# A layered kernel on one core: the routed layer chooses its experts by raw logits, and steps and dataless matmuls are placed anew

## The chip, the core and the metric

One Trainium2 chip, of which the kernel uses 1 core. The metric is the device time of one execution in microseconds (us). Before the change it is 2814.28 us, the median of 3 runs (2812.36 to 2824.87).

The engines are named PE (TensorE, matmuls; PEld is its weight load), DVE (VectorE), ACT (ScalarE), POOL (GpSimd) and SP (SyncE, here only DMA issues).

## What is computed

For each of 16 sequences of 256 tokens by 128 features, two layers with two parts each: a selective scan, a routed feed-forward part, a gated delta rule, and attention with a dense mixture of 8 experts. The change is in the routed part:

```
logits = X @ routing_W.T + expert_bias            # 8 per token
activation = sqrt(softplus(logits))
top_vals, top_idx = top_k(activation, 2)
combine = sum(one_hot(top_idx) * top_vals)        # 8 coefficients per token, two of them not zero
hdn = silu(X @ rW1[e] + rb1[e]);  y = hdn @ rW2[e] + rb2[e]
out = shared(X) + sum_e combine[e] * y[e]
```

Softplus and square root both rise with their argument, so the two largest activations belong to the two largest logits.

## The kernel before, in words

A sequence is one item: its 256 tokens are two tiles of 128 partitions. The work of an item is a list of named steps in two halves. The first half (x) has the scan (names a_), the routed part (b_) and the projections of the delta rule (c_norm to c_roots). The second half (y) has the delta rule's pair products (c_logd, c_prod), the inversion of two triangular blocks in five levels (lev_T, lev_Z, lev_TT, each for two chunks), its application (c_R to c_res), the attention (d_) and the experts (d_up, d_down, d_mix).

`follow` runs the first half of item 0 alone, then a loop of 15 iterations, each with the first half of item i and the second half of item i-1 interleaved, and then the second half of the last item alone. Every engine has its own program and keeps its own strict order. In the loop the order is a string of x and y, `TURNS`: each letter takes the next step of its half. Engines wait for one another through semaphores (`Signal`, with `at(i, k)` as the count to wait for).

`WARM` names steps of PE ahead of which `keep_warm` issues that many matmuls of constants into a bank that nobody reads, before the step's first wait. They compute nothing that is used.

Steps that matter here. On the DVE: `b_logits2` (L1416) adds the bias to the logits and makes -|x| for the softplus; `softplus16` (L1298) makes log(1+exp(-|x|)) in 13 small dependent steps, each waiting for the one before, after ACT's exp; `b_select` (L1423) takes the largest values (`max`), their indices (`max_index`), turns them to floats, and makes the 8 coefficients from four picks and a sum; `b_coef` copies the turned coefficients. On POOL `b_root_` (L560) takes the square root of all 16 softplus columns as a power, and `power` (L530) makes the roots of the norms. Both `b_` and the delta rule's `c_beta`/`c_soft2` use the same softplus code.

The order of the DVE around it: c_rms, b_logits, b_soft2, c_gated, b_select, c_res, b_coef, d_norm. PE's: b_logits, c_turn_o (turns what c_gated made), c_out (projects it; c_res needs it), b_coef (turns the coefficients), b_up. ACT copies between c_turn_o and c_out.

Of the kernel before, what the change touches and what calls it, by code (L numbers as in the profile page):

```python
# [9 lines left out]
ALU = mybir.AluOpType  # L10
# [15 lines left out]
E0 = 8  # L26
# [88 lines left out]
for e in range(E1):  # L115
    EXPERTS += [("d_down", e, 0), ("d_down", e, 1)]
    if e + 2 < E1:
# [11 lines left out]
        "yyyyyxyxyyyyyyxxyyyyyxyyyyxyxyyyxyxyyyyxxyyyxxyyxxyyxxyxyxxyxxxxyxyxxyyxxxxyxxxyyxyyyxyyxyyxxyyy"  # L129
        "yyxyxyyyyxyyxyyxyyxyyxyyyxxyyyxxxyyyyyyyxx"),  # L130
    "vector": (
        "xyxyyyxyyxyyxyyyyxxyyyxyyxyyxyyxyyxyyxyyxyyxyyxxyxyxxxyxyxxxxxxyxyxxyxyxxyxyxyxxyxxxyxyyxxxyyyxy"
        "xxxyxxxxyxyxxxyxyxxyyyy"),
    "scalar": (
        "yyxxyyxxxxxyyyxyyyyyxxyyxyyxyxxxyxxyxxxyxxyyyxyxyyxxyxyxyyxyyxxyyxyxyxxxyyxyxyxyyxxx"),
    "gpsimd": (
        "yyxxyyyyyyxxxxxxxxxxyyxyxxx"),
# [4 lines left out]
    ("a_xproj",): 2, ("a_out",): 2, ("b_turn",): 1, ("b_logits",): 1, ("c_prod", 2, 0): 1, ("c_prod", 2, 1): 1,  # L142
    ("lev_Z", 0, 0): 2, ("lev_TT", 0, 0): 2, ("lev_Z", 1, 0): 1, ("lev_TT", 1, 0): 2, ("lev_TT", 1, 1): 1,
    ("lev_Z", 2, 1): 2, ("lev_TT", 2, 0): 1, ("lev_TT", 2, 1): 2, ("lev_Z", 3, 1): 2, ("lev_TT", 3, 0): 2,
    ("lev_TT", 3, 1): 1, ("lev_Z", 4, 1): 1, ("lev_TT", 4, 0): 3, ("lev_TT", 4, 1): 1, ("c_X", 0): 3, ("c_O", 0): 1,
    ("c_S",): 1, ("c_kS",): 1, ("c_top", 1): 1, ("c_low", 1): 1, ("c_O", 1): 2, ("c_turn_o",): 2, ("c_out",): 1,
    ("d_scores",): 2, ("d_turn_p",): 1, ("d_av",): 1, ("d_a",): 2,
# [16 lines left out]
def build(nc, a, out, NB):  # L164
    with ExitStack() as ctx:
# [107 lines left out]
        topf = sb("topf", [P, TILES, 8])  # L273
        pick = sb("pick", [P, TILES, 2, E0])
# [99 lines left out]
        b_lgp = sig("b_logits_ps"); b_lg = sig("b_logits"); b_sel = sig("b_select", 4); b_root = sig("b_root")  # L374
# [19 lines left out]
        c_tp = sig("c_top_ps", 2); c_tx = sig("c_top", 2); c_lp = sig("c_low_ps", 2); c_low = sig("c_low", 2)  # L394
        c_X = sig("c_X_ps", 2); c_U = sig("c_U", 2); c_Uw = sig("c_Uw")
# [4 lines left out]
        d_qk = sig("d_qk_ps"); d_qks = sig("d_qk", 2); d_vp = sig("d_v_ps"); d_v = sig("d_v")  # L400
# [113 lines left out]
        def _(g):  # L514
# [94 lines left out]
        def _(s):  # L609
# [58 lines left out]
            def sp_exp(i, which):  # L668
                s.wait_ge(sp_in.h, sp_in.at(i, which + 1))
                s.activation(sp[:, 1, :], sp[:, 1, :], ACT.Exp).then_inc(sp_e.h, 1)  # L670
# [133 lines left out]
        def _(t):  # L804
# [246 lines left out]
            def c_top(i, ch):  # L1051
# [10 lines left out]
                last.then_inc(c_tp.h, 1)  # L1062

            def c_low_(i, ch):
# [6 lines left out]
                last.then_inc(c_lp.h, 1)  # L1071

            def c_X_(i, ch):
# [5 lines left out]
                last.then_inc(c_X.h, 1)  # L1079
# [130 lines left out]
        def _(v):  # L1210
# [205 lines left out]
            def b_logits2(i):  # L1416
# [4 lines left out]
                softplus16_in(i, 0, lg2)  # L1421

            def b_select(i):  # L1423
                v.wait_ge(b_root.h, b_root.at(i, 1))
# [4 lines left out]
                v.wait_ge(b_sel.h, b_sel.at(i, 1))  # L1429
                v.tensor_copy(*carrier)  # L1430
# [41 lines left out]
            def c_beta(i):  # L1472
# [5 lines left out]
                softplus16_in(i, 1, lg2)  # L1478
# [5 lines left out]
            def c_soft2(i):  # L1484
                softplus16(i, 1, lg2)
# [101 lines left out]
            def c_low_(i, ch):  # L1587
                v.wait_ge(c_lp.h, c_lp.at(i, ch + 1))
# [158 lines left out]
```

## Time and profile before

| | |
|---|---|
| median of 3 runs | 2814.28 us |
| the profiled execution | 2817.26 us, span 2815.5 us |
| mean granted TensorE clock | 0.931 |
| PE busy | 2434.8 us (86%), 22584 matmuls |
| DVE busy | 2208.3 us (78%) |
| ACT busy | 1197.7 us (43%) |
| POOL busy | 605.6 us (22%) |

The span is the time from the first to the last instruction. The clock is given as a share of full speed: 1.00 is 2.4 GHz, 0.50 is 1.2 GHz. A line of a timeline has the start in us from the span's start, the time in us, engine, line of the kernel, operation, what is written and read, how many such instructions follow one another (a line with x4 merges four), and in brackets how long the engine sat idle before it and who released it. The loop's iterations are all alike, so one of them is read, the one whose DVE part starts at 1171.60 us.

### The profile page before, as it was taken

The page shows a single profiled execution, that of the slowest core. Times are in us where ns is not written, and L with a number is a line of the kernel's source. Part 1 is how long each engine was busy: PE and PEld are TensorE (multiplying, and loading weights), DVE is VectorE, ACT ScalarE, POOL GpSimd, SP SyncE. Part 2 cuts the span into 40 slices and gives each one's busy share as a digit, 9 for nine tenths or more (in the row PEclk, how much of TensorE's full clock was granted, in tenths as well). Part 3 has the DMA queues.
Part 4 walks back from the last instruction along what each step waited for, and adds up shares of the span by engine and source line. Part 5 has one row for each costly group of instructions (what it writes and reads, how often), then busy time and mean ns, then how long its engine had stood idle before and what let it go on. Part 6 is the DMA issues. An engine that isn't in the chain of part 4 may idle for free.

```text
span 2815.5 us, 60867 instructions
## 1 busy us (share of the span) xinstructions
PE 2434.8 (86%) x22584; PEld 1890.6 (67%) x22584; DVE 2208.3 (78%) x5056; ACT 1197.7 (43%) x2697; POOL 605.6 (22%) x465
## 2 busy tenths in 40 slices
PE   4688989888898888989888898988889888898987
PEld 2466767667686766768667686766768666676875
DVE  6677887878879787887978779787887978788742
ACT  3233536435263542536444253543526354353612
POOL 2122221221322122231222222122131212223100
PEclk7689999989999999999999999999999999999987
DMA  4000000000000000000000000000000000000000
GB/s 132 4 2 3 7 4 1 8 3 7 3 7 2 3 8 3 7 4 1 8 3 8 3 7 4 1 8 3 7 3 7 2 3 8 3 7 2 1 6 2
DMA packets 24831, 21.41 MB, mean 8 GB/s; under 512 B 7217, under 2 KB 21570, under 8 KB 24530
## 3 DMA queue, kind: packets, MB, share of 16 engines
q1 hardware_dynamic: 24530, 17.26, 2.2%
q8 instruction: 205, 3.36, 0.5%
q14 instruction: 96, 0.79, 0.1%
HBM read 15.13 MB, written 2.13 MB: 6 GB/s over the span
## 4 chain that ended last, share of the span: by engine, by line
issue 42%; PE 25%; DVE 23%; POOL 6%; ACT 1%; DVEq 0%; POOLq 0%; ACTq 0%
PE banks L1048 4%; PE banks L887 3%; PE banks L1020 3%; DVE wide L1390 3%; PE banks L1012 2%; DVE wide L1398 2%; DVE inv L1560 2%; POOL lg L562 2%; DVE inv L1564 2%; DVE wide L1378 2%; POOL rq L534 2%; PE banks L1001 1%; PE banks L1040 1%; DVE inv L1551 1%; PE banks L864 1%
## 5 line engine op out<-in xcount | busy, mean ns | idle before, releaser
L558 POOL TENSOR_TENSOR wide<-wide 128x512 f32<-128x512 f32 x128 | 215.3, 1682 | 782.0 <-DVE wide L1398 428.4
L1513 DVE SCALAR_TENSOR_TENSOR wide<-pad,conv,wide 128x256 f32<-128x256 f32 x864 | 369.5, 492 | 0.0
L1390 DVE TENSOR_TENSOR_SCAN wide<-wide 128x1024 f32<-128x1024 f32 x128 | 294.3, 2300 | 1.9 <-ACT wide L664 0.3
L1040 PE MATMUL banks<-hideb,identb 128*128 128x512 bf16 x800 | 276.1, 402 | 0.0
L1184 PE MATMUL banks<-inv,up 128*128 128x256 f32 x1024 | 265.9, 391 | 0.0
L1194 PE MATMUL banks<-down,inv 128*128 128x128 f32 x2048 | 257.2, 277 | 0.0
L1194 PEld LDWEIGHTS banks<-down,inv 128*128 128x128 f32 x2048 | 250.7, 192 | 5.9
L1020 PEld LDWEIGHTS banks<-inv 64*64 64x64 f32 x5120 | 164.4, 136 | 111.4 <-issue 111.4
L792 ACT ACTIVATE inv<-banks,up1b 128x256 f32<-128x256 f32 x512 | 206.7, 481 | 65.0 <-PE banks L1184 63.3
L1020 PE MATMUL banks<-inv 64*64 64x64 f32 x5120 | 182.2, 222 | 57.8 <-DVE inv L1564 57.8
L664 ACT ACTIVATE wide<-small,a_neg 128x255 f32<-128x255 f32 x512 | 214.4, 496 | 35.7 <-DVE wide L1390 35.5
L1184 PEld LDWEIGHTS banks<-inv,up 128*128 128x128 f32 x1024 | 184.6, 193 | 21.0 <-issue 0.2
L745 ACT COPY inv<-banks 128x512 f32<-128x512 f32 x160 | 91.3, 580 | 242.0 <-DVE inv L1560 209.5
L1020 PEld LDWEIGHTS banks<-inv,mats 64*64 64x64 f32 x5120 | 163.8, 136 | 35.4 <-issue 35.4
L1020 PE MATMUL banks<-inv,mats 64*64 64x64 f32 x5120 | 180.6, 221 | 4.6 <-DVE inv L1557 4.6
L1378 DVE TENSOR_TENSOR wide<-banks,small 128x1024 f32<-128x1024 f32 x128 | 154.2, 1205 | 3.4 <-PE banks L864 3.4
L534 POOL TENSOR_TENSOR vscale<-vscale,expo 128x16 f32<-128x16 f32 x16 | 46.3, 2895 | 506.8 <-DVE rq L1522 506.8
L1398 DVE TENSOR_TENSOR wide<-banks,wide 128x1024 f32<-128x1024 f32 x128 | 154.2, 1204 | 1.0
L1689 DVE SCALAR_TENSOR_TENSOR inv<-banks,gt,inv 128x128 f32<-128x128 f32 x256 | 77.1, 342 | 98.9 <-PE banks L1194 98.9
L864 PE MATMUL banks<-bc,sel3b 96*128 96x256 bf16 x512 | 100.5, 285 | 55.9 <-DVE wide L1378 31.4
L968 PEld LDWEIGHTS banks<-ones_col,wide 128*128 128x128 f32 x1024 | 135.0, 200 | 9.4 <-issue 2.2
L887 PE MATMUL banks<-wide,con 128*128 128x512 f32 x256 | 138.6, 634 | 0.3 <-POOL wide L558 0.3
(277 smaller groups left out, 4846.7 us busy)
## 6 DMA issues: line engine op xcount, KB each, us to landing
gates_bc<-gate_rows SPq DMA_DIRECT2D x32, 128.0 KB, 2.9
x<-in_x SPq DMA_DIRECT2D x16, 128.0 KB, 2.1
up<-in_W SPq DMA_DIRECT2D x1, 2048.0 KB
out<-xn_y SPq DMA_DIRECT2D x16, 128.0 KB, 2.0
wide<-in_wmod SPq DMA_DIRECT2D x2, 384.0 KB, 5.3
con<-in_con SPq DMA_DIRECT2D x1, 724.0 KB, 4.5
w_k<-in_Wk SPq DMA_DIRECT2D x1, 512.0 KB
w_q<-in_Wq SPq DMA_DIRECT2D x1, 512.0 KB
```

The costliest lines, as they stand in the source:

```text
L558: g.tensor_tensor(ypart[p % 2], r[:, 0:512], r[:, 512:1024], ALU.add).then_inc(a_yp.h, 1)
L664: last = s.activation(decay[st % 2][:, at + 1:at + T], dt[:, c, 1:T], ACT.Exp, scale=a_neg[:, c, st * SG + q:st * SG + q + 1])
L792: s.activation(hm[e % 2][:, m, :], bank(3 + half, T, q * T), ACT.Relu, bias=up1b[:, HB1 * e + m:HB1 * e + m + 1]).then_inc(d_hid.h, 1)
L887: t.matmul(bank(2), ident, ypart[st % 2], start=st == 2, stop=st == NG + 1).then_inc(a_yq.h, 1)
L1020: last = t.matmul(PS[a:b, out, h * HALF:(h + 1) * HALF], weights(h, a, b), values(h, a, b), start=True, stop=True)
L1040: t.matmul(bank(bk), identb[:], hideb[:].unsqueeze(1).broadcast_to([P, HG, P]), start=True, stop=True)
L1184: last = t.matmul(bank(3 + half, T, q * T), up1[:, e, m * P:(m + 1) * P], xxT, start=True, stop=True)
L1194: last = t.matmul(bank(bk, D, j * D), hm[e % 2][:, m, j * P:(j + 1) * P], down1[:, HB1 * e + m, :], start=m == 0, stop=m == HB1 - 1)
L1378: v.tensor_tensor(drive[st % 2].rearrange("p (q c t) -> p q c t", q=SG, c=CB), bank(0).rearrange("p (q t) -> p q t", t=T).unsqueeze(2).bro ...
L1390: v.tensor_tensor_scan(state[st % 2], decay[st % 2], drive[st % 2], 0.0, ALU.mult, ALU.add).then_inc(a_h.h, 1)
L1398: v.tensor_tensor(r, bank(1).rearrange("p (q t) -> p q t", t=T).unsqueeze(2).broadcast_to([P, SG, CB, T]), r, ALU.mult).then_inc(a_rd.h, 1)
L1513: v.scalar_tensor_tensor(dst, src, w, dst, ALU.mult, ALU.add).then_inc(c_conv.h, 1)
```

## The change

The routed part's softplus and root are no longer taken of all 16 logits of a partition (2 tiles x 8), but of the 4 chosen ones (2 x 2). `max` is run on the logits themselves in `b_logits2`; the two largest of each tile are copied into `chosen`, whose -|x| goes to ACT; the indices are found and made floats in the same step, ahead of the softplus. The softplus steps take their width as an argument (4 here, 16 for the delta rule as before). POOL's power writes 4 values into `topv`, and `b_select` keeps only picks and sum.

`TURNS` and `WARM` are new for all engines: 50 dataless matmuls per iteration become 45. A few semaphores are merged (`c_slv` for `c_tp`, `c_lp`, `c_X`; `d_qkv_ps` for two), with the same events behind each wait.

```diff
             def b_root_(i):
-                g.tensor_tensor(lg[:]..., sp[:, 0, :], expo[:, 1:2].broadcast_to([P, TILES * E0]),
+                g.tensor_tensor(topv[:]..., sp[:, 0, 0:2 * TILES], expo[:, 1:2].broadcast_to([P, 2 * TILES]),
...
             def b_logits2(i):
                 v.wait_ge(b_lg.h, b_lg.at(i, 1))
-                softplus16_in(i, 0, lg2)
-
-            def b_select(i):
-                v.wait_ge(b_root.h, b_root.at(i, 1))
                 v.tensor_copy(*carrier)
                 for j in range(TILES):
                     last = v.max(top[:, j, :], lg[:, j, :])
                 last.then_inc(b_sel.h, 1)
                 v.wait_ge(b_sel.h, b_sel.at(i, 1))
+                v.tensor_copy(chosen[:].rearrange("p (j n) -> p j n", n=2), top[:, :, 0:2]).then_inc(b_sel.h, 1)
+                v.wait_ge(b_sel.h, b_sel.at(i, 2))
+                softplus_in(i, 0, chosen[:], 2 * TILES)
                 v.tensor_copy(*carrier)
                 for j in range(TILES):
                     last = v.max_index(topi[:, j, :], top[:, j, :], lg[:, j, :])
                 last.then_inc(b_sel.h, 1)
-                v.wait_ge(b_sel.h, b_sel.at(i, 2))
+                v.wait_ge(b_sel.h, b_sel.at(i, 3))
                 v.tensor_copy(topf[:], topi[:]).then_inc(b_sel.h, 1)
-                v.wait_ge(b_sel.h, b_sel.at(i, 3))
+
+            def b_select(i):
+                v.wait_ge(b_root.h, b_root.at(i, 1))
+                v.wait_ge(b_sel.h, b_sel.at(i, 4))
                 for j in range(TILES):
                     for n in range(2):
-                        last = v.tensor_scalar(pick[:, j, n, :], ..., topf[:, j, n:n + 1], top[:, j, n:n + 1],
+                        last = v.tensor_scalar(pick[:, j, n, :], ..., topf[:, j, n:n + 1], topv[:, j, n:n + 1],
                                                ALU.is_equal, ALU.mult)
```

What the new strings do to the order of the loop, engine by engine (steps not named keep their places):

```
DVE   start:      c_prod 0 1 ahead of a_norm2; a_zgate ahead of c_prod 2 1, a_silu2 ahead of c_prod 3 1
      inversion:  before: a_split a_soft Z00 Z01 T10 a_step T11 Z10 scan0 Z11 T20 read0 T21 Z20 scan1 ...
                  after:  a_split Z00 Z01 a_soft T10 T11 Z10 Z11 a_step T20 T21 scan0 Z20 read0 Z21 T30 scan1 ...
      attention:  d_v ahead of b_up 4
      end:        d_mix 4 behind c_scales
PE    inversion:  scan0 behind TT11 (was behind Z10), read0/scan1 behind TT20, read1/scan2 behind TT30
      attention:  d_turn ahead of b_up 2, d_qkv ahead of b_up 3, d_scores ahead of b_up 5
      end:        d_down 5 1 ahead of c_turn_k 1; c_turn_v ahead of d_down 7
ACT   inversion:  x_kept and the level 0 copy of chunk 0 ahead of a_soft; its chunk 1 ahead of scan0 and scan1
      later:      scan7 ahead of c_S; d_turn and d_qkv one step earlier among b_up
POOL  no step that has work is moved
```

(Z01 is lev_Z of level 0, chunk 1; T is lev_T and TT is lev_TT.)

The counts of `WARM` that change, per iteration: fewer at a_xproj, a_out, c_O 1, d_scores (2 to 1 each), c_X 0 (3 to 1), c_kS and d_turn_p (1 to 0), c_turn_o (2 to 0), lev_Z 0 0, 2 1 and 3 1 (2 to 1), lev_Z 4 1 (1 to 0), lev_TT 0 0 and 1 0 (2 to 0), 2 1 and 3 0 (2 to 1), 4 0 (3 to 2); more at b_turn (1 to 2), c_X 1 and c_turn (0 to 1), d_turn and c_prod 3 1 (0 to 2), lev_Z 0 1 (0 to 2), 1 0 (1 to 2), 2 0 and 4 0 (0 to 1), 3 0 (0 to 3), lev_TT 3 1 (1 to 2).

## Rows read from the trace of the kernel before

**Rows 1.** Windows by stage: us, busy of PE, PEld, DVE, ACT, POOL, clock, DMA.

```profile
1190.00:1226.00 36.00, 30.26 (x662) 22.85 (x662) 34.81 (x45) 17.13 (x34) 3.82 (x3) 1.00 0.01 3
...
1290.00:1310.00 20.00, 20.00 (x126) 18.07 (x125) 19.49 (x57) 16.94 (x43) 1.45 (x1) 1.00 0.00 1
```

**Rows 2.** Timeline of the DVE, the logits (L1418) of five items.

```profile
421.14 0.17 DVE L1418 TENSOR_TENSOR lg<-banks,rout_b 128x16 f32<-128x16 f32 x1 [1.83 <-PE banks L906]
...
589.60 0.17 DVE L1418 TENSOR_TENSOR lg<-banks,rout_b 128x16 f32<-128x16 f32 x1 [1.36 <-PE banks L906]
...
758.19 0.17 DVE L1418 TENSOR_TENSOR lg<-banks,rout_b 128x16 f32<-128x16 f32 x1 [1.58 <-PE banks L906]
...
924.80 0.17 DVE L1418 TENSOR_TENSOR lg<-banks,rout_b 128x16 f32<-128x16 f32 x1 [1.58 <-PE banks L906]
...
2597.19 0.17 DVE L1418 TENSOR_TENSOR lg<-banks,rout_b 128x16 f32<-128x16 f32 x1 [1.58 <-PE banks L906]
```

**Rows 3.** Windows at the low clock (0.50), columns as in rows 1.

```profile
667.60:670.90 3.30, 3.20 (x6) 1.72 (x7) 0.96 (x6) 0.60 (x1) 0.25 (x1) 0.50 0.20 50
756.40:766.40 10.00, 5.05 (x19) 3.32 (x19) 5.42 (x29) 1.36 (x3) 6.30 (x2) 0.50 0.00 0
...
1258.10:1271.60 13.50, 8.86 (x28) 5.67 (x29) 8.90 (x42) 1.69 (x4) 6.47 (x3) 0.50 0.00 0
```

**Rows 4.** Timeline of the DVE, logits to coefficients.

```profile
1259.08 0.17 DVE L1418 TENSOR_TENSOR lg<-banks,rout_b 128x16 f32<-128x16 f32 x1 [1.58 <-PE banks L906]
...
1259.74 0.17 DVE L1308 TENSOR_SCALAR sp<-sp 128x16 f32<-128x16 f32 x1 [0.28 <-ACT sp L670]
...
1263.27 0.69 DVE L1631 TENSOR_TENSOR inv<-inv,gnw 128x512 f32<-128x512 f32 x1
1266.02 0.15 DVE L1425 COPY carried<-con 128x1 f32<-128x1 f32 x1 [2.06 <-POOL lg L562]
...
1267.03 0.87 DVE L1439 TENSOR_SCALAR pick<-con,topf,top 128x8 f32<-128x8 f32 x4
1267.93 0.18 DVE L1443 TENSOR_TENSOR cf<-pick 128x16 f32<-128x16 f32 x1
```

**Rows 5.** Timeline of POOL, three powers.

```profile
1254.25 0.71 POOL L534 TENSOR_TENSOR mv_x<-mv_x,expo 128x2 f32<-128x2 f32 x1 [6.04 <-DVE mv_x L1265]
...
1257.58 2.90 POOL L534 TENSOR_TENSOR rms<-rms,expo 128x16 f32<-128x16 f32 x1 [1.01 <-DVE rms L1623]
1262.59 3.40 POOL L562 TENSOR_TENSOR lg<-sp,expo 128x16 f32<-128x16 f32 x1 [2.10 <-DVE sp L1318]
```

**Rows 6.** Timeline of PE, c_turn_o, c_out and b_coef.

```profile
1264.01 1.11 PE L1104 MATMUL banks<-con,inv 128*128 128x128 f32 x4 [4.10 <-DVE inv L1631]
...
1265.80 2.08 PE L1112 MATMUL banks<-w_o,inv 128*128 128x128 f32 x8 [0.25 <-ACT inv L757]
1268.17 0.60 PE L929 MATMUL banks<-con,cf 128*9 128x128 f32 x2 [0.29 <-DVE cf L1443]
```

**Rows 7.** Timeline of PE, between b_out and d_turn_p.

```profile
1281.99 0.39 PE L1040 MATMUL banks<-hideb,identb 128*128 128x512 bf16 x1
1282.21 0.60 PE L1137 MATMUL banks<-con,inv 128*128 128x128 f32 x4
```

**Rows 8.** Timeline of PE, c_turn_v at the loop's end.

```profile
1334.05 0.60 PE L984 MATMUL banks<-con,wide 128*128 128x128 f32 x4
```

**Rows 9.** Timeline of the DVE, the last d_mix and the loop's restart.

```profile
1334.34 0.61 DVE L1689 SCALAR_TENSOR_TENSOR inv<-banks,gt,inv 128x128 f32<-128x128 f32 x2 [1.18 <-PE banks L1194]
...
1338.83 0.49 DVE L1259 BATCH_NORM_STATS2 stats_x<-x 128x6 f32<-128x128 f32 x2 [2.58 <-issue]
```

**Rows 10.** Timeline of the DVE, the loop's start and the inversion's first level.

```profile
1173.64 0.59 DVE L1271 TENSOR_SCALAR xn_x<-x,mv_x 128x128 f32<-128x128 f32 x2
...
1176.30 0.61 DVE L1541 SCALAR_TENSOR_TENSOR mats<-banks,negc,inv 128x128 f32<-128x128 f32 x2 [0.30 <-PE banks L1012]
...
1196.15 0.72 DVE L1560 STREAM_TRANSPOSE inv<-banks 128x512 f32<-128x512 f32 x1 [0.73 <-PE banks L1020]
```

More of the change, by code:

```diff
@@ L128 @@
     "tensor": (
-        "yyyyyxyxyyyyyyxxyyyyyxyyyyxyxyyyxyxyyyyxxyyyxxyyxxyyxxyxyxxyxxxxyxyxxyyxxxxyxxxyyxyyyxyyxyyxxyyy"
-        "yyxyxyyyyxyyxyyxyyxyyxyyyxxyyyxxxyyyyyyyxx"),
+        "yyyyyxyxyyyyyyxxyyyyyyyyxyyyxxyyyyxxyyxyxyyyxxyyxxyyxxyxyxxyxxxxyxyxxyyxxxyxyxxyxxyyyxyyxyyxxyyy"
+        "yyxxyyyyyxyyxyyxyyxyyxyyyxyxyyxxyxyyyyxyyx"),
     "vector": (
-        "xyxyyyxyyxyyxyyyyxxyyyxyyxyyxyyxyyxyyxyyxyyxyyxxyxyxxxyxyxxxxxxyxyxxyxyxxyxyxyxxyxxxyxyyxxxyyyxy"
-        "xxxyxxxxyxyxxxyxyxxyyyy"),
+        "xyyxyyxyxyyxyyyyyxyyxyyyyxyyxyxyyxyxyyxyxyyxyyxxyxyxxxyxyxxyxxxxxyxxyxyxxyxyxyxxyxxyxxyyxxxyyyxy"
+        "xxxyxxxxyxyxxxxyxxyyyyy"),
     "scalar": (
-        "yyxxyyxxxxxyyyxyyyyyxxyyxyyxyxxxyxxyxxxyxxyyyxyxyyxxyxyxyyxyyxxyyxyxyxxxyyxyxyxyyxxx"),
+        "yyxxyyxxyyxyxxyyxyxyyyxyyyxxxyyxxxxyxxyxyxxxyyyxyyxxyxyxyyxyyxyxxyxyxyyxyxyxyxxyyxxx"),
     "gpsimd": (
-        "yyxxyyyyyyxxxxxxxxxxyyxyxxx"),
+        "yyxyyyyyyxxxxxxxxxxxyyxyxxx"),
 }
 WARM = {
[L142 to L147, printed above, removed]
+    ("a_xproj",): 1, ("a_out",): 1, ("b_turn",): 2, ("b_logits",): 1, ("c_turn",): 1, ("c_prod", 2, 0): 1,
+    ("c_prod", 2, 1): 1, ("c_prod", 3, 1): 2, ("lev_Z", 0, 0): 1, ("lev_Z", 0, 1): 2, ("lev_Z", 1, 0): 2,
+    ("lev_TT", 1, 1): 1, ("lev_Z", 2, 0): 1, ("lev_Z", 2, 1): 1, ("lev_TT", 2, 0): 1, ("lev_TT", 2, 1): 1,
+    ("lev_Z", 3, 0): 3, ("lev_Z", 3, 1): 1, ("lev_TT", 3, 0): 1, ("lev_TT", 3, 1): 2, ("lev_Z", 4, 0): 1,
+    ("lev_TT", 4, 0): 2, ("lev_TT", 4, 1): 1, ("c_X", 0): 1, ("c_O", 0): 1, ("c_S",): 1, ("c_top", 1): 1,
+    ("c_low", 1): 1, ("c_X", 1): 1, ("c_O", 1): 1, ("c_out",): 1, ("d_turn",): 2, ("d_scores",): 1, ("d_av",): 1,
+    ("d_a",): 2,
 }
@@ L669, in sp_exp @@
                 s.wait_ge(sp_in.h, sp_in.at(i, which + 1))
-                s.activation(sp[:, 1, :], sp[:, 1, :], ACT.Exp).then_inc(sp_e.h, 1)
+                n = (2 * TILES, TILES * NH)[which]
+                s.activation(sp[:, 1, 0:n], sp[:, 1, 0:n], ACT.Exp).then_inc(sp_e.h, 1)
             def b_up_(i, m):
@@ L1078, in c_X_ @@
                     last = t.matmul(PS[HALF:P, 3 + ch, h * DV:(h + 1) * DV], TTd[ch][HALF:P, h, :], R[HALF:P, h, :], start=True, stop=True)
-                last.then_inc(c_X.h, 1)
+                last.then_inc(c_slv.h, 1)
             def c_O_(i, ch):
@@ L1698, in _ @@
                            b_norm=lambda i: norm(i, 1), b_norm2=lambda i: norm2(i, 1), b_logits=b_logits2,
-                           b_soft2=lambda i: softplus16(i, 0, lg2), b_select=b_select, b_coef=b_coef, b_up=b_up_, b_res=b_res,
+                           b_soft2=lambda i: softplus(i, 0, chosen[:], 2 * TILES), b_select=b_select, b_coef=b_coef, b_up=b_up_, b_res=b_res,
                            c_norm=lambda i: norm(i, 2), c_norm2=lambda i: norm2(i, 2), c_beta=c_beta, c_soft2=c_soft2,
```

52 lines of the change are left out of this document (27 added, 25 removed).

## The prediction

> **What bounds the kernel now.** I read the DVE and PE timelines of one period of the loop first, then the same period in windows by stage. In the inversion stage the DVE is busy 34.81 of 36.00 us, in the experts' stage PE is busy for all of 20.00 us and the DVE for 19.49 [rows 1]. So the DVE sets the pace from the loop's start to the end of the scan, PE sets it through the experts, and in the 30 us between the two a chain of small steps does: logits, softplus, root, choice, residual, attention. The reader is to see that an order changed inside a stage whose bound has no idle time can only keep or lose time.
>
> Second, the start of the routed layer's logits (L1418) in each iteration [rows 2]. From the 5th to the 15th iteration of the loop it comes (2597.19 - 924.80) / 10 = 167.24 us apart, while 421.14 to 589.60 is 168.46 and 758.19 to 924.80 is 166.61. Third, where TensorE's clock is at its low level, 1.2 GHz [rows 3]: in a settled iteration it is low through 1258.1 to 1271.6, from just before the logits; the short iteration of 166.61 had its low stretch from 756.4 for only 10.0 us, 1.8 us before its logits; an early, long one had a second low stretch at 667.6. My reading: the place of an iteration against the clock's steps decides how much of its work is slow, and lateness is partly given back. That is worth up to 167.24 - 166.61 = 0.63 us per iteration.
>
> The sentences on a page: the Trainium skill, "TensorE: Matmul & The Clock Gate", section "Part 1: The HAM clock gate (the "warmup" mystery)", says that the activity window that decides the clock runs free of the kernel. The steady 167.24 after unequal first periods agrees; taken as a strict rule it would hold the loop at exactly 167.24, which is the second rival below.
>
> **The change part by part.**
>
> Routed choice, before: logits at 1259.08, softplus steps from 1259.74 (0.28 of it a wait for ACT's exp), c_gated ends at 1263.27 + 0.69 = 1263.96, the DVE then waits 2.06 for the root and runs the choice from 1266.02 to 1267.93 + 0.18 = 1268.11 [rows 4]. After: maximum, index and cast (1267.03 - 1266.02 = 1.01) move ahead of the softplus steps, with one new small copy; a small dependent step is about 0.21 from start to start, so logits, copy and minus-absolute value are 0.63. Softplus starts 1.64 after the logits instead of 0.66: 0.98 later, and ACT's exp hides in it. Its 13 steps get 4 columns for 16. No row of before has these steps at 4 columns; the bounds are 0 and, for lack of a nearer row, a saving of 0.02 each, and I take 0.01, 0.1 in all. c_gated thus ends 0.9 later, at 1264.86.
>
> The power on POOL: 16 columns take 2.90 where nothing disturbs it and 3.40 here, 2 columns 0.71 [rows 5]. For 4 I take an estimate on the line between, 0.71 + 2 x 2.19 / 14 = 1.0 (bounds 0.7 and 2.9). It runs beside c_gated's 1.4, so the 2.06 wait vanishes. Of the choice, picks and sum are left, 1268.11 - 1267.03 = 1.08: the coefficients are ready at 1265.95, 2.15 earlier.
>
> What is late next: PE turns c_gated's result (1.11), ACT copies it, c_out takes 2.08 and ends at 1267.88; then PE waited 0.29 for the coefficients [rows 6]. All of this now ends 0.9 later, 1268.78. On the DVE c_res stands between choice and b_coef and waits for c_out: it starts at 1268.80 instead of 1268.11, and b_coef and d_norm behind it. So the 2.15 gained turns into 0.7 lost here. Two things give it back: PE has no gap before b_coef any more, so the high clock may come back earlier, and d_turn and d_qkv are put ahead of b_up's later blocks. I walk it through the rows to b_out, which needs the last hidden block: it starts within 0.3 of where it did. I take 0; bounds -0.5 (clock back earlier) and +0.7.
>
> The dataless matmuls: ahead of d_turn_p the one at 1281.99, between b_out's end and the turn at 1282.21, goes: -0.2 on the path [rows 7]. The others lie in PE's waits; around c_kS, c_X and c_O a few of about 0.22 each are freed on PE where the DVE is the bound: 0. Whether their new places keep the clock high I can't price from before; it is the slower rival.
>
> The loop's end: the last d_down is followed by c_turn_v (four turns, 0.60, about 0.44 from start to start) [rows 8]; now c_turn_v goes first. The last d_mix starts as its matmuls end and the DVE restarts at 1338.83, with 2.58 of loop overhead, behind it [rows 9]. PE has no gap there, so the restart is 0.44 later: +0.4 (bounds 0 and 0.6).
>
> The loop's start: a_norm2 (1173.64) now follows one more c_prod step, 0.9 later; the wait of 0.30 at 1176.30, a PE product held up by that very step, partly pays for it. The convolution waits for the chain a_norm2, turn, a_in: +0.3 (bounds 0 and 0.9) [rows 10].
>
> The inversion: before, scan work filled the gaps between levels and the DVE waited 0.73 once (1196.15) [rows 10]. Now levels 0 and 1 run through before the scan begins. The 0.73 is what one such gap costs when a single transpose (0.72) stands where PE has a level's product to make. With nothing but the other chunk's transpose to cover it I take two gaps of 0.5 and 0.4 for level 1, estimates below that row. On ACT a_soft is now queued behind the copy for level 0, which waits for the DVE's transpose of level 1, so exp and log come later, and a_step waits for them, by another 0.4. 1.3 instead of 0.7: +0.6 (bounds -0.7, were all idle gone, and +1.2). The fused semaphores wait for the same events: 0. ACT's scans are in time for the DVE either way.
>
> Sum per iteration: 0 - 0.2 + 0.4 + 0.3 + 0.6 = +1.1, before the clock gives back 0.6: +0.5. Fifteen iterations of the loop: +7.5. Ahead of the loop the first routed layer runs alone, without c_gated behind the root: the change saves 3.4 - 1.0 there, some 2.5 once. After the loop, new places of dataless matmuls: 0, bounds -4 and +4. The profiled execution, span 2815.5, own time 2817.26, becomes 2822.3; the median of the runs stands 2.98 below it, so 2819.3, say 2819.
>
> **The rivals.**
>
> The choice's gain passes. If c_gated's chain is not last (PE at its high clock for c_turn_o and c_out: 1.11 + 2.08 would halve) and the new order of the inversion costs nothing, 2.15 per iteration goes: -32 - 2.5 gives 2780; half of it, 2797. For it: the root's wait is the longest of the DVE in that stage. Against: c_out ended only 0.2 before the DVE came to it.
>
> The loop holds its step. Periods return to 167.24 whatever the stages do, and only the first part's 2.5 is gained: 2812. For it: ten periods average 167.24 after three unequal ones [rows 2]. Against: a give-back of more than 0.63 was never seen.
>
> Slower: new low stretches. With the 50 dataless matmuls cut to 45 and put elsewhere, PE goes to its low level in a second place, as at 667.6 [rows 3], in every iteration. Price: 168.46 - 167.24 = 1.2 per iteration on top of the 0.5, or in place of the give-back: 1.2 to 2.3 times 15, +18 to +34, less 2.5: 2830 to 2846. It decides as soon as one such stretch stands in each period of the loop, or if my +1.1 isn't given back at all (+16.5 - 2.5: 2828).
>
> **How the numbers follow.** Forecast 2819 (its own range 2809 to 2827) 0.35; loop holds its step 0.20; slower 0.27; choice's gain passes 0.18. The bound of 0.5% (about what a measurement of this kernel can tell from no change) is 14 us: 2800 and 2828. Faster 0.18; same 0.54; slower 0.28, with a little of the forecast's upper end. For 8 in 10 the range takes in half of the faster case and most of the slower one: 2793 to 2838.
>
> **What would show it.** Right: no DVE wait at the routed choice; the DVE waits for PE (c_out) before c_res; waits of 0.3 to 0.5 behind the first transposes of level 1; a_soft's exp behind a copy on ACT; the last d_mix later by 0.4 from PE's last d_down; logits 167.2 to 167.8 apart. Wrong: logits under 166.5 apart with c_res starting at once (the gain passes), or a 0.50 stretch outside the one round the logits in a settled iteration (the slower rival). A power of 4 columns on POOL longer than 1.4 would bring back a wait ahead of the picks.

## The result, and the profile after

The changed kernel takes 2852.84 us, the median of 4 runs (2852.45 to 2857.18), beside 2813.34 us of the kernel before (4 runs, 2812.36 to 2824.87): ratio 1.0129, 95% interval 1.0108 to 1.0150. It is 1.3% slower where 0.2% was forecast, and beyond the range's upper end of 2838. The profiled execution took 2852.45 us.

The page of after, its span and the engines' busy time:

```profile
span 2850.7 us, 60783 instructions
...
PE 2441.0 (86%) x22504; PEld 1899.2 (67%) x22504; DVE 2216.5 (78%) x5072; ACT 1194.4 (42%) x2697; POOL 586.2 (21%) x465
```

Shares say nothing here: the DVE's busy time rose by 8 us and the span by 35. So I read one settled period of the loop, logits to logits, on the DVE, as before. Columns: start, time, engine, line, operation, and in brackets the idle time before and its releaser.

```profile
1442.31 0.17 DVE L1422 TENSOR_TENSOR lg<-banks,rout_b 128x16 f32<-128x16 f32 x1 [1.17 <-PE banks L910]
...
1443.68 0.16 DVE L1312 TENSOR_SCALAR sp<-sp 128x4 f32<-128x4 f32 x1
...
1446.99 0.69 DVE L1637 TENSOR_TENSOR inv<-inv,gnw 128x512 f32<-128x512 f32 x1
...
1447.94 0.87 DVE L1445 TENSOR_SCALAR pick<-con,topf,topv 128x8 f32<-128x8 f32 x4 [0.27 <-POOL topv L565]
...
1451.74 0.42 DVE L1290 TENSOR_TENSOR xn_y<-banks,gates_bc 128x256 f32<-128x256 f32 x1 [2.71 <-PE banks L1116]
...
1517.65 0.61 DVE L1695 SCALAR_TENSOR_TENSOR inv<-banks,gt,inv 128x128 f32<-128x128 f32 x2 [1.61 <-PE banks L1198]
...
1521.83 0.49 DVE L1263 BATCH_NORM_STATS2 stats_x<-x 128x6 f32<-128x128 f32 x2 [2.65 <-issue]
...
1525.56 1.73 DVE L1275 TENSOR_SCALAR xn_x<-x,mv_x 128x128 f32<-128x128 f32 x2
...
1549.77 0.69 DVE L1570 TENSOR_TENSOR inv<-banks,con 128x512 f32<-128x512 f32 x1 [0.73 <-PE banks L1024]
1550.71 0.69 DVE L1570 TENSOR_TENSOR inv<-banks,con 128x512 f32<-128x512 f32 x1 [0.24 <-PE banks L1024]
1551.56 0.69 DVE L1370 SCALAR_TENSOR_TENSOR small<-small 128x512 f32<-128x512 f32 x1 [0.17 <-ACT small L655]
...
1612.66 0.17 DVE L1422 TENSOR_TENSOR lg<-banks,rout_b 128x16 f32<-128x16 f32 x1 [1.17 <-PE banks L910]
```

The period is 1612.66 - 1442.31 = 170.35, against 167.24 in [rows 2]. Of the routed choice, the 2.06 us wait of [rows 4] is now 0.27, for POOL; but c_res, the next step shown, waits 2.71 for PE's c_out (L1116). c_gated ends 1446.99 + 0.69 - 1442.31 = 5.37 after the logits, against 4.88 in [rows 4]. The line to stop at is a_norm2 (L1275): its two instructions took 0.59 in [rows 10] and take 1.73. POOL's timeline of after, the power in the choice and then what stands beside a_norm2:

```profile
1446.31 1.51 POOL L565 TENSOR_TENSOR topv<-sp,expo 128x4 f32<-128x4 f32 x1 [2.19 <-DVE sp L1322]
...
1525.57 0.64 POOL L596 TENSOR_SCALAR_AFFINE_SELECT mats<-mats 128x512 f32<-128x512 f32 x1 [1.61 <-DVE mats L1547]
1526.18 1.04 POOL L584 TENSOR_TENSOR inv<-gl,con 128x512 f32<-128x512 f32 x1
```

Windows at the low clock in the same period (start:end, length, busy of PE, PEld, DVE, ACT, POOL, clock, DMA, GB/s):

```profile
1442.60:1452.60 10.00, 4.62 (x17) 3.34 (x17) 6.37 (x33) 0.79 (x2) 3.02 (x2) 0.50 0.00 0
1521.10:1524.40 3.30, 3.30 (x9) 2.62 (x8) 1.90 (x9) 0.60 (x1) 1.02 (x3) 0.50 0.05 12
1586.00:1589.20 3.20, 3.20 (x14) 2.61 (x13) 3.20 (x3) 1.08 (x3) 2.43 (x1) 0.50 0.03 5
```

In [rows 3] a settled iteration had one such stretch, round the logits. Now there are three: round the logits (shorter, 10.0 for 13.5 us), at the loop's restart, 79 us after the logits, and behind c_X 0, 144 us after them. Of the 14 full periods 11 have both the second and the third, and the other three have one in the inversion, 113 to 114 us after the logits.

The rest is told by stage. The table is worked out from the starts of DVE instructions in each trace, as medians over the 14 periods between the item 1 and item 15 logits. "prob" is the first step that uses the attention's probabilities, "split" is a_split. "Low stretch" is short for a stretch at the low clock. A second number behind a slash is the value in periods that have no further low stretch in that stage.

| kernel | period | logits to c_res | to prob | to last d_mix | to restart | to split | to c_R 0 | to logits |
|---|---|---|---|---|---|---|---|---|
| before | 167.30 | 9.03 | 12.49 / 11.95 | 53.97 | 4.19 | 18.95 | 34.98 | 33.55 |
| changed | 170.37 | 9.43 | 11.50 | 54.69 | 3.93 | 20.96 / 20.26 | 35.43 | 34.30 / 33.55 |
| e1_choice_only | 167.74 | 9.42 | 12.15 / 11.90 | 53.97 | 4.20 | 18.96 | 34.98 | 33.55 |
| e3_old_warm | 169.56 | 9.42 | 11.62 | 54.73 | 3.81 | 21.20 / 20.26 | 35.58 | 33.54 |
| f1_end_order | 167.30 | 9.38 | 11.90 | 54.54 | 3.97 | 18.95 | 34.99 | 33.56 |
| f2_inversion_order | 168.59 | 9.43 | 11.90 | 53.98 | 4.31 | 19.02 / 18.95 | 35.58 | 33.56 |
| g1_start_order | 170.28 | 9.42 | 11.90 | 53.97 | 4.22 | 21.28 / 20.26 | 36.10 | 33.15 |
| h2_changed_apart | 169.00 | 9.43 | 11.50 | 54.69 | 3.81 | 20.23 / 19.12 | 35.61 | 33.55 |
| h3_filled_inversion | 165.57 | 8.05 | 11.90 | 53.97 | 4.21 | 19.26 | 35.00 | 33.15 |

For before, the value behind the slash is that of periods whose low stretch round the logits is 10 us long and not 13.5. The 14 periods from the second logits to the last take 2383.57 us for 2344.70 (+38.9, or 2.8 each). What lies ahead of the second logits is 1.6 shorter, the tail behind the last 2.1, and 38.9 - 3.7 is the span's 35.2.

### The profile page after: what moved, and what is told of

The parts are those of the page before. It is cut to its first block, busy times and chain, and to the rows that moved or that the text cites. A ratio compares the mean times of both kernels' runs of the same rounds, so it can differ in the third digit from the quotient of the medians.

```text
span 2850.7 us, 60783 instructions
## 1 busy us (share of the span) xinstructions
PE 2441.0 (86%) x22504; PEld 1899.2 (67%) x22504; DVE 2216.5 (78%) x5072; ACT 1194.4 (42%) x2697; POOL 586.2 (21%) x465
## 4 chain that ended last, share of the span: by engine, by line
issue 38%; DVE 27%; PE 26%; POOL 4%; ACT 2%; DVEq 0%; POOLq 0%; ACTq 0%
PE banks L1052 4%; DVE wide L1394 3%; PE banks L891 3%; DVE wide L1402 3%; DVE inv L1566 2%; PE banks L1188 2%; PE banks L1198 2%; PE banks L1016 2%; DVE inv L1570 2%; DVE wide L1382 2%; DVE xn_x L1275 2%; POOL rq L537 1%; PE banks L1024 1%; DVE inv L1557 1%; DVE mats L1547 1%
## 5 line engine op out<-in xcount | busy, mean ns | idle before, releaser
L561 POOL TENSOR_TENSOR wide<-wide 128x512 f32<-128x512 f32 x128 | 226.0, 1766 | 778.6 <-DVE wide L1402 435.8
L1044 PE MATMUL banks<-hideb,identb 128*128 128x512 bf16 x720 | 260.3, 398 | 0.0
L1016 PE MATMUL banks<-kq 128*128 128x256 f32 x512 | 148.7, 424 | 0.1
```

Source lines behind the costliest of these rows:

```text
L561: g.tensor_tensor(ypart[p % 2], r[:, 0:512], r[:, 512:1024], ALU.add).then_inc(a_yp.h, 1)
L1044: t.matmul(bank(bk), identb[:], hideb[:].unsqueeze(1).broadcast_to([P, HG, P]), start=True, stop=True)
```

## The experiments

Each ratio is to the kernel before, run beside it on the same chip, with a 95% interval.

### Choice, orders and dataless matmuls taken apart

```diff
 e1_choice_only:  the changed kernel
-TURNS, WARM as changed
+TURNS, WARM as before
```

> The kernel before with the routed choice of the change alone: max on the raw logits, softplus and root on 4 columns, the old order of steps and the old dataless matmuls. Theory A (the new orders and the moved dataless matmuls cost the time, the choice is nearly neutral because c_gated's chain is 0.5 to 0.9 us later): within 6 us of before, periods of the loop 167.2 +- 0.2, no low-clock stretch outside the one round the logits. Theory B (the later c_gated alone pushes the loop out of its 167.24 us step): about 2850, periods near 170.6 with extra low-clock stretches. Theory C (the choice's 2.06 us wait is a real gain): 2785 or less, periods 165.5 or less.

```diff
 e2_orders_only:  the kernel before
-TURNS, WARM as before
+TURNS, WARM as changed
```

> The kernel before with the new order strings and the new counts of dataless matmuls, but the old choice (16 columns, root before the choice). Theory A: as slow as the changed kernel, 2845 to 2860, periods near 170.6, low-clock stretches at the loop's restart and in the application stage. Theory B (the choice is the cause): within 6 us of before. If choice and orders were tuned for each other: slower than the changed kernel by 2 us per iteration, 2880.

```diff
 e3_old_warm:  the changed kernel
-WARM as changed
+WARM as before
```

> The changed kernel with the old counts of dataless matmuls (50 for 45), new order and new choice kept. If the moved dataless matmuls let the clock fall (c_X 0 has 3 again where the changed kernel has a low stretch after it): the stretch after c_X 0 is gone, and the time falls towards 2815 to 2830. If the order of steps is the cause: within 6 us of the changed kernel, 2852.

```diff
 e4_old_turns:  the changed kernel
-TURNS as changed
+TURNS as before
```

> The changed kernel with the old order of steps, the new counts of dataless matmuls and the new choice kept. If the order of steps is the cause: within 6 us of before, 2813. If the dataless matmuls are the cause: a low-clock stretch after c_X 0 in each period and 2835 to 2855. If either alone is enough, both this and the kernel with the old counts stay near 2850; if only both together do it, both come out near 2813.

| kernel | median us | before beside it | ratio |
|---|---|---|---|
| e1_choice_only | 2818.60 | 2817.10 | 1.0004 (0.9989 to 1.0018) |
| e2_orders_only | 2850.25 | 2817.10 | 1.0110 (1.0085 to 1.0136) |
| e3_old_warm | 2847.52 | 2817.10 | 1.0102 (1.0077 to 1.0126) |
| e4_old_turns | 2860.99 | 2817.10 | 1.0152 (1.0128 to 1.0177) |

The new choice alone changes nothing that can be measured; everything lost comes from the orders and the dataless matmuls. e1's periods are not as even as its text expected: 5 of 14 have a low stretch at the restart and take 168.1 to 168.6, and 2 have one in the inversion. e3 and e4 met neither of their expectations either: e3 has the stretch behind c_X 0 in only 2 of 14 periods and is as slow all the same, and e4 is slower than expected, with that stretch in only 2 of 14. Each of these two loses on its own: new orders with the old dataless matmuls cost 1.0% (e3), new dataless matmuls under the old orders 1.5% (e4), and together they cost less than e4 alone. So the new counts fit the new orders, but orders with their own counts are still 1.1% behind (e2). Under the old orders (e4) the stretch from split to c_R 0 is 36.99 for 34.98: 36.65 in the three periods without a low stretch in it, so 1.67 is the new counts' own price under the old order, and 36.9 to 37.1 in the 11 with one. Another low stretch stands at the restart in all 14.

Why the choice is neutral stands in e1's DVE timeline:

```profile
1423.11 0.17 DVE L1421 TENSOR_TENSOR lg<-banks,rout_b 128x16 f32<-128x16 f32 x1 [1.58 <-PE banks L909]
...
1428.74 0.87 DVE L1444 TENSOR_SCALAR pick<-con,topf,topv 128x8 f32<-128x8 f32 x4 [0.27 <-POOL topv L564]
...
1432.52 0.42 DVE L1289 TENSOR_TENSOR xn_y<-banks,gates_bc 128x256 f32<-128x256 f32 x1 [2.71 <-PE banks L1115]
```

The picks start 5.63 after the logits; in [rows 4] it was 1267.03 - 1259.08 = 7.95. Then the DVE waits 2.71 for c_out, and c_res comes 0.4 later than before. By prob the 0.4 is gone again in the medians, 21.57 for 21.52 from the logits.

### The moved steps, one stage at a time

f1, f2 and g1 are e1_choice_only with only the order of one stage taken from the change; g2 is the changed kernel with one step put back.

```diff
 f1_end_order, PE from c_proj to c_decay, DVE from c_proj to the last d_mix
-PE   c_proj 10, d_up 6 0 ... c_turn_k 1, d_down 5 1 ... d_down 7, c_turn_v
+PE   d_up 6 0, c_proj 10 ... d_down 5 1, c_turn_k 1 ... c_turn_v, d_down 7
-DVE  d_mix 3, c_proj 10, d_mix 4 ... c_scales
+DVE  c_proj 10, d_mix 3 ... c_scales, d_mix 4
```

> The kernel with the new choice alone (old orders, old dataless matmuls; it ran level with before) plus the new order at the loop's end: c_turn_v ahead of d_down 7, d_down 5 1 ahead of c_turn_k 1, d_up 6 0 ahead of c_proj 10, d_mix 4 behind c_scales. Theory S (costs of the stages add up, as in the prediction): logits to the next restart 0.4 us longer, +6 us over the loop, about 2822. Theory N (the step before c_turn_v was not at its bound): no longer, within 5 us of before.

Measured 2822.86 us beside 2820.35, ratio 1.0015 (0.9992 to 1.0038). To the last d_mix 0.57 more, to the restart 0.23 less: +0.34. Yet the settled periods are 167.07 to 167.45, as in before (167.06 to 167.39): the 0.34 and c_res's 0.35 are taken back between c_res and prob, where before spends 12.5 us in 10 periods and f1 11.90. With it the low stretch round the logits is 10 us long and not 13.5, so this is the clock giving back, and here it covers all. The size of the added work doesn't tell when that happens: e1, with the 0.4 of c_res alone, is at 167.74.

```diff
 f2_inversion_order, DVE from a_split to scan 3, PE from lev_Z 1 0 on, ACT from a_xproj to b_turn
-DVE  a_split a_soft Z00 Z01 T10 a_step T11 Z10 scan0 Z11
+DVE  a_split Z00 Z01 a_soft T10 T11 Z10 Z11 a_step T20 T21 scan0
```

> The kernel with the new choice alone plus the new order of the inversion on DVE, PE and ACT (levels 0 and 1 ahead of the scan, ACT's later scans too). Theory S: the stretch from a_split to c_R 0 is 0.5 us longer (predicted 0.6; the changed kernel showed 0.44), 15 times, and periods without a further low stretch 167.8: about 2820 to 2828. Theory W (the inversion order carries most of the 1.6 us by which the new orders' undisturbed periods exceed the old): periods without a further low stretch 168.5 or more, 2835 or more.

Measured 2828.83 us beside 2820.35, ratio 1.0038 (1.0014 to 1.0062), just above the 2820 to 2828 expected. From split to c_R 0 it is 35.58 for 34.98: +0.60, nine us in the loop. Its DVE timeline has the waits for PE's products of one level:

```profile
1365.82 0.69 DVE L1567 TENSOR_TENSOR inv<-banks,con 128x512 f32<-128x512 f32 x1 [0.74 <-PE banks L1021]
1366.76 0.69 DVE L1567 TENSOR_TENSOR inv<-banks,con 128x512 f32<-128x512 f32 x1 [0.24 <-PE banks L1021]
```

Before waited once, 0.73 [rows 10]; here the 0.74 is followed by one of 0.24 and by 0.17 for ACT, as in the changed kernel.

```diff
 g1_start_order, DVE from c_prod 0 0 to a_split
-a_norm2, c_prod 0 1;  c_prod 2 1, a_zgate;  c_prod 3 1, a_silu2
+c_prod 0 1, a_norm2;  a_zgate, c_prod 2 1;  a_silu2, c_prod 3 1
```

> The kernel with the new choice alone (old dataless matmuls) plus the new order of the DVE at the loop's start: c_prod 0 1 ahead of a_norm2, a_zgate ahead of c_prod 2 1, a_silu2 ahead of c_prod 3 1. Theory P (a_norm2 now starts together with POOL's unit diagonal and mask, which wait for that same c_prod step, and one of the two engines is held up): restart to a_split 20.2 us for 18.95, a_norm2's two instructions 1.7 us for 0.6, about 2838 to 2846. Theory S (as predicted, only the delay of 0.9 us less what the waits give back): 19.25, about 2822.

```diff
 g2_norm_back, the changed kernel, DVE
-c_prod 0 1, a_norm2
+a_norm2, c_prod 0 1
```

> The changed kernel with one step moved back on the DVE: a_norm2 ahead of c_prod 0 1. Theory P: a_norm2 0.6 us again, restart to a_split at least 0.9 us shorter in periods with the same low stretches (18.9 to 19.2 where the clock is high at the restart), total about 2830 to 2840. If the clock's further low stretches carry the 170.4 us by themselves: within 5 us of the changed kernel.

g1: 2856.05 us beside 2816.64, ratio 1.0124 (1.0082 to 1.0167): the start's order alone costs as much as the whole change, and 10 us more than was expected. In its trace a low stretch stands at the restart in 12 of 14 periods and one in the inversion in all 14, which makes split to c_R 0 36.10 for 34.98. g2: 2831.73 beside 2816.64, ratio 1.0050 (1.0032 to 1.0067): one step moved back one place, in the whole changed kernel, returns 21 us. From restart to split it is 20.26 with the new order in the periods that no low stretch disturbs, and 18.95 with a_norm2 back, so the moves of a_zgate and a_silu2, which g2 keeps, cost nothing here.

The row that shows how is in e3's trace, a period without a low stretch at the restart, so the clock is no part of it. DVE, then POOL:

```profile
1350.19 0.49 DVE L1262 BATCH_NORM_STATS2 stats_x<-x 128x6 f32<-128x128 f32 x2 [2.53 <-issue]
...
1353.08 1.74 DVE L1274 TENSOR_SCALAR xn_x<-x,mv_x 128x128 f32<-128x128 f32 x2
...
1370.45 0.25 DVE L1348 CAST bc<-small 96x256 bf16<-96x256 f32 x1
...
1353.08 0.64 POOL L595 TENSOR_SCALAR_AFFINE_SELECT mats<-mats 128x512 f32<-128x512 f32 x1 [0.76 <-DVE mats L1546]
1353.69 1.04 POOL L583 TENSOR_TENSOR inv<-gl,con 128x512 f32<-128x512 f32 x1
```

a_split (the cast) starts 1370.45 - 1350.19 = 20.26 after the restart. a_norm2 and POOL's select start at the same 1353.08, because both come right behind the DVE's c_prod 0 1. POOL's two instructions end at 1354.73, and a_norm2's pair, 0.59 long in [rows 10], ends at 1354.82. Taken apart, the pair's first instruction takes 0.72 and ends at 1353.80, just behind POOL's select (1353.08 + 0.64); its second takes 1.09, from 1353.72, and ends just behind POOL's mask.

### Only POOL's work moved

If contention (the two engines holding each other up) and not the order is what costs, the new order must become cheap when only POOL's work is moved.

```diff
 h1_start_order_apart (on g1) and h2_changed_apart (on the changed kernel), POOL's c_unit
                 g.wait_ge(c_MT.h, c_MT.at(i, 4 * gr + 4))
+                if gr == 0 and not isinstance(i, int):
+                    g.wait_ge(ln_x[0].h, ln_x[0].at(i + 1, 1))       # a_norm2's result
```

> The kernel with the new choice and the new DVE order at the loop's start (2856), in which POOL's first unit diagonal (and with it the second mask behind it) also waits for a_norm2's result, so that the two can't run at once; the DVE's order is the same. Theory P (the two engines hold each other up): a_norm2's two instructions 0.6 us instead of 1.7, restart to a_split 19.0 to 19.4 where no low stretch stands, 2820 to 2835. Theory D (the delay of a_norm2 by one step is enough): restart to a_split still 20.2 or more, 2845 or more.

> The changed kernel with that same wait on POOL and nothing else. Theory P: like the changed kernel with a_norm2 moved back (2832), 2828 to 2842. Theory D: within 5 us of the changed kernel.

h1: 2836.15 us beside 2817.76, ratio 1.0059 (1.0036 to 1.0081), 20 us less than g1 and 1 above its expected range. h2: 2831.04 beside 2817.76, ratio 1.0038 (1.0017 to 1.0060), 22 us less than the changed kernel. h2's trace, DVE and POOL:

```profile
1346.32 0.59 DVE L1277 TENSOR_SCALAR xn_x<-x,mv_x 128x128 f32<-128x128 f32 x2
...
1347.41 0.61 DVE L1549 SCALAR_TENSOR_TENSOR mats<-banks,negc,inv 128x128 f32<-128x128 f32 x2 [0.49 <-PE banks L1018]
...
1347.16 0.64 POOL L598 TENSOR_SCALAR_AFFINE_SELECT mats<-mats 128x512 f32<-128x512 f32 x1 [2.52 <-DVE xn_x L1277]
1347.77 1.04 POOL L584 TENSOR_TENSOR inv<-gl,con 128x512 f32<-128x512 f32 x1
```

The DVE's order is the changed one in both, a_norm2 takes 0.59 again, and split comes 19.12 after the restart for 20.26. So of the start's +1.31, 1.14 is contention between DVE and POOL, and 0.17 is the order itself, with POOL's new wait in it. It matters which DVE step stands beside POOL: in h2 the same two POOL instructions run beside c_prod (1347.41), which takes 0.61 as in [rows 10]. Not all comes back: h1 is still 18 us behind before. A low stretch stands at the restart in 13 of its 14 periods and in the inversion in 9, and in the one period without the first, split comes 19.13 after the restart. The Trainium skill, "SBUF — State Buffer", section "SBUF: two separate sides", says of the port pair that DVE and GpSimd share that it is "an exclusive lock, not a bandwidth split". The trace agrees: the DVE's pair ends as POOL's ends (1354.82 and 1354.73) instead of both going at half pace.

### Dataless matmuls at the low stretches

```diff
 f3_changed_kept_high, the changed kernel
-c_X 0: 1, c_low 0: 0
+c_X 0: 4, c_low 0: 2, and at the loop body's end:  keep_warm(3, "restart")   # restart: 8
```

> The changed kernel with 8 dataless matmuls more at the very end of the loop's body, c_X 0 raised from 1 to 4 and c_low 0 from 0 to 2, meant to keep TensorE's clock high at the restart and after c_X 0. Theory C (the two further low stretches of each period cost about 1.1 and 0.8 us): both stretches gone, periods near 168.8, about 2825 to 2832. Theory O (the order alone sets the time): periods still above 170, 2845 or more.

Measured 2844.47 us beside 2820.35, ratio 1.0095 (1.0060 to 1.0130). The low stretches at the restart and behind c_X 0 are gone; one at 113 us after the logits, in the inversion, came in 10 of 14 periods. That gives back 8 us of 39 by the medians, where 2825 to 2832 was expected if those two stretches were what costs. The filling has its own price: restart to split is 20.72 where the undisturbed value is 20.26, c_R 0 to the logits 34.09 for 33.55, so most of what the clock gives is spent on the matmuls that keep it up. Keeping the clock up doesn't mend the order. The stretch behind c_X 0 stands in 2 of 14 periods of e3 and in none of f3, which have 3 and 4 dataless matmuls there, and in 11 of 14 of the changed kernel, with 1. The count doesn't decide alone: e4 has 1 there too, and the stretch in 2 of 14; 11 of the other 12 have one in the inversion instead.

### Does the choice pay at the high clock?

```diff
 f4_choice_filled (on e1), g3_before_filled (on before)
-b_turn: 1, b_logits: 1, c_turn_o: 2
+b_turn: 9, b_logits: 3, c_turn_o: 20, restart: 8
 g4_choice_filled_less:  f4 with restart: 3
 h4_filled_five:         f4 with restart: 5
 h3_filled_inversion:    h4 with
+                    keep_warm(7, "a_scan", st)                      # a_scan 0: 6
                     t.wait_ge(a_drv.h, a_drv.at(i, st + 1))
```

> The kernel with the new choice alone (old orders) plus dataless matmuls that fill PE's waits round the logits: 9 before b_turn, 3 before b_logits, 20 before c_turn_o, and 8 at the end of the loop's body. If the low clock round the logits is what makes c_turn_o and c_out (1.11 and 2.08 us) stand in the way of the choice's gain: no low stretch in the loop, c_out in about 1.0, periods 164 to 165.5, 2765 to 2790. If not the clock but the chain itself holds: periods 166.5 or more, 2800 or more.

> The kernel before (old choice, old orders) with the same dataless matmuls added as in the filled kernel with the new choice (2798): 9 before b_turn, 3 before b_logits, 20 before c_turn_o, 8 at the end of the body. If the high clock alone brought that kernel its gain: within 5 us of it, 2793 to 2803. If the new choice pays once c_turn_o and c_out run at the high clock (logits to c_res 8.05 there, while the old choice can't be below 9.0 because the DVE waits 2.06 for the root): 15 x 1.0 us slower than it, 2810 to 2820.

> The filled kernel with the new choice, with 3 instead of 8 dataless matmuls at the end of the body. There the restart to a_split took 19.4 to 19.8 us for 18.95: if the 8 ran into PE's first products of the next period, 18.95 to 19.1 again and periods 165.2 to 165.8, 2785 to 2792; if 3 are too few to keep the clock high at the restart, low stretches there and periods 166.5, 2800.

> The new choice, old orders, dataless matmuls 9 before b_turn, 3 before b_logits, 20 before c_turn_o, 5 at the end of the body and 6 in PE's wait for the first drive of the scan. If the low stretches left in the filled kernels (at the restart with 3, in the inversion with 8) are what keeps their periods at 166.4 to 166.8: no low stretch left, periods 165.2 to 165.6, 2780 to 2788. If the 6 delay the inversion's products: a_split to c_R 0 above 35.3 us, 2795 or more.

> The same without the 6 in the inversion. Expected between the two filled kernels measured: restart to a_split 19.0 to 19.3, some low stretches in the inversion (0.6 us each), periods 165.3 to 166.2, 2785 to 2795.

| kernel | median us | before beside it | ratio |
|---|---|---|---|
| f4_choice_filled | 2798.12 | 2820.35 | 0.9927 (0.9901 to 0.9954) |
| g3_before_filled | 2810.07 | 2816.64 | 0.9973 (0.9957 to 0.9988) |
| g4_choice_filled_less | 2792.11 | 2816.64 | 0.9906 (0.9867 to 0.9946) |
| h4_filled_five | 2796.14 | 2817.76 | 0.9895 (0.9859 to 0.9931) |
| h3_filled_inversion | 2786.36 | 2817.76 | 0.9862 (0.9823 to 0.9902) |

f4 fell between its two expectations: c_out takes 1.16 for 2.08, but 9 of 14 periods have a low stretch in the inversion. g4, with 3 at the restart, has one at the restart in 8 of 14, and h4, with 5, in 3 of 14.

With the same filling, the new choice is 12 us faster than the old by the medians (f4 and g3, ratios 0.9927 and 0.9973). From logits to c_res the old choice takes 9.04 at the high clock and 9.03 at the low one: root and choice are last there, whatever PE does. The new one takes 9.42 at the low clock and 8.05 at the high one. The difference of 0.99 times 15 is 15 us, near the 12.

h3 has the lowest median of all: 1.4% faster than before. Of that, the 12 us between f4 and g3 (about 0.4%) are shown to be the choice's; the kernel before with h3's filling wasn't run. h3's trace; DVE, then PE round the choice, then one window nearly a period long:

```profile
1408.78 0.17 DVE L1452 TENSOR_TENSOR lg<-banks,rout_b 128x16 f32<-128x16 f32 x1 [1.17 <-PE banks L939]
...
1416.83 0.42 DVE L1320 TENSOR_TENSOR xn_y<-banks,gates_bc 128x256 f32<-128x256 f32 x1 [1.33 <-PE banks L1146]
...
1408.60 4.48 PE L1074 MATMUL banks<-hideb,identb 128*128 128x512 bf16 x20
...
1415.54 1.16 PE L1146 MATMUL banks<-w_o,inv 128*128 128x128 f32 x8 [0.46 <-ACT inv L789]
...
1408.80:1574.20 165.40, 152.65 (x1450) 116.86 (x1449) 137.21 (x316) 74.60 (x168) 35.94 (x29) 1.00 0.02 5
```

The 20 dataless matmuls (L1074) fill PE's wait for c_gated, c_out takes 1.16 where it took 2.08 [rows 6], and the clock is 1.00 through the whole window, as in 13 of the 14 periods. Whether 3, 5 or 8 at the restart is best these intervals don't tell.

## Why the prediction was wrong

**Steps that held.** The coefficients: 2.15 earlier against the logits was forecast, they came 2.31 earlier (6.72 after the logits for 9.03). c_res +0.7 with the DVE waiting for c_out: measured +0.40, direction and cause right. It was put too high because the softplus steps begin 1.37 after the logits where 1.64 was reckoned, so that c_gated ends 0.49 later for 0.9. That the attention gives it back: from logits to prob the changed kernel takes 9.43 + 11.50 = 20.93; before, in a period with the same 10 us low stretch, 9.03 + 11.95 = 20.98, so -0.05 for a forecast of 0; in periods with the short low stretch, c_res to prob is 11.50, where e1 and f1 have 11.90: the new orders with the old counts bring 0.28 of this (e3, 11.62), the new counts the rest. d_turn_p: e4, with the old orders and without that dataless matmul, has 53.80 from prob to the last d_mix for 53.97, -0.17 for -0.2. The end: +0.34 alone (f1) for +0.4, and in the changed kernel 54.69 + 3.93 - 53.97 - 4.19 = +0.46 with d_turn_p in it, for +0.2. The inversion: +0.60 alone, +0.45 with the new dataless matmuls, for +0.6. The first routed layer, alone ahead of the loop: its coefficients come 6.19 after its logits for 8.60, -2.4 for -2.5; the tail is 2.1 shorter, for 0 with bounds of 4.

**A bound that was right and an estimate that wasn't.** POOL's power of 4 columns, put at 1.0, takes 1.51 beside c_gated. The prediction named 1.4 as the point from which a wait before the picks comes back; it did, 0.27. Nothing hangs on it, as c_out is later.

**The step that failed first: the loop's start.** It was put at +0.3 with bounds 0 and 0.9 and measured +1.31 where the clock is undisturbed, outside its own bounds. The argument followed a_norm2 against its neighbours on the DVE and against PE, and never asked what starts on POOL at the same moment. POOL's select and mask wait for c_prod 0 1, and the change puts a_norm2 exactly behind that step. h1 and h2 show that this is what costs: with POOL's work alone moved, 20 and 22 us are back, and the start is +0.17 (h2), within the bounds that were given. The stage sum without further low stretches is then 9.43 + 11.50 + 54.69 + 3.93 + 20.26 + 35.43 + 33.55 = 168.79 per period. It is a sum of stages from different periods, as each of the 14 has a further low stretch somewhere. Against before's 166.62 in its short period that is +2.17 for the forecast +1.1, and the start accounts for 1.0 of the 1.07 missed.

**The step that failed second: what the clock makes of it.** The forecast let the clock give 0.6 back and put the rest at +0.5. The first half happened: the low stretch round the logits is 10.0 us for 13.5, and c_res to prob lost its 0.54. Then 168.79 - 167.30 = +1.49 was left. But the loop did not stay there: most periods are 170.2 to 170.9, with low stretches at the restart (0.5 to 1.5 more before split) and behind c_X 0 (0.75 to 0.9 more). That is the slower rival. It had 0.27 and a price of 1.2 to 2.3 per iteration; against before it was 38.9 / 14 = 2.8, because two stretches stood in most periods and not one, on top of a sum that was already 1.0 too low. The condition it was given was right, a 0.50 stretch outside the one round the logits; the trace shows two.

**The rivals.** That the choice's gain passes fell, under the condition it named: at the low clock c_out is last. At the high clock it passes, by 0.99 and not 2.15, since c_out is still last (1.33 of wait in h3). That the loop holds its step fell for this change, though f1 shows it for a small one. The Trainium skill, "TensorE: Matmul & The Clock Gate", section "Part 1: The HAM clock gate (the "warmup" mystery)", has the window run free of the kernel; the prediction's strict reading of it would have kept the loop at 167.24, and the changed kernel's 170.37 speaks against that reading.

**Open.** Why a low stretch comes at the restart in 12 and behind c_X 0 in 11 of 14 periods of the changed kernel, and in 5 and none of e1, is not settled. PE is busy through both (3.30 of 3.30 and 3.20 of 3.20 us). Just ahead of the restart's first product PE idles for 1.60 us, but in before it idles 1.63 at the same place and the clock stays high; and no run tells which of PE's work ahead of the stretches brings them on. That the start's delay shifts the loop against the clock's steps is only argued: h2, with the delay gone, is at 169.00 and not at 167.3, and h1, which has only the start's order on top of e1 and no contention, at 169.43 where e1 is at 167.74. How the losses of e3 and e4 fit together, 1.0% and 1.5% and not more in both, wasn't taken apart further.

## What to carry to other kernels

When a step is moved on one engine, look at what the other engines release from the same event: a DVE step put right behind the producer that POOL waits for starts together with POOL's work, and half a microsecond of work can become nearly two. Price a stage in periods that the clock doesn't disturb and the clock's stretches apart from it. The size of a delay doesn't tell what the clock makes of it: 0.34 at the end of the loop was given back whole (f1), while 0.17 at its start came with a low stretch more in nearly every period (h1). A shorter chain pays only where it is last: here it took dataless matmuls in PE's waits beside it to turn a neutral choice into a gain of some 12 us.

## What the runs showed of the hardware that was not expected

- Two DVE TENSOR_SCALAR of 128x128 take 0.59 us alone and 1.73 when they start together with two POOL instructions of 0.64 and 1.04 us; those two take 0.64 and 1.04 either way. Beside these two the DVE alone pays. The order of events is that of taking turns: each DVE instruction ends 0.08 us behind the POOL instruction that it overlaps (e3).
- A POOL power of 4 columns takes 1.007 us in the first part, where the DVE has nothing beside it, and 1.51 beside c_gated on the DVE, where 2 columns took 0.71 and 16 took 2.90 and 3.40 [rows 5]. The row of after, minimum, median and maximum in ns:

```profile
L565 POOL TENSOR_TENSOR topv<-sp,expo x16: 1007/1511/1513, 92.7 to 2638.4; 128x4 f32<-128x4 f32 x16
```

- A loop's period can stay the same over more work while the clock's low stretch shrinks: before and f1_end_order both settle at 167.1 to 167.5 with 0.69 us more work on the path in f1, and a low stretch of 10 us for 13.5. With the clock at 2.4 GHz through the period (h3) it is 165.4 to 165.9.
